# A fused gated-scan and mixture-of-experts kernel on one core: low half 2 moved ahead of VectorE's block turn, the second norm split between GpSimd and ScalarE, and the statistics of x moved behind the tokens' low half

## What is computed

```python
x = x + layernorm(attn(layernorm(x)))        # block 1
x = x + layernorm(ffn(layernorm(x)))         # block 2

# attn: g = sigmoid(x Wg^T + bg); h[l] = (1-g[l])*h[l-1] + g[l]*x[l]; h Wo^T + bo
# ffn:  each token is routed to one of 8 experts, argmax(softmax(x router_w + router_b));
#       an expert takes at most C = 320 of its tokens (rank < C), which get
#       relu(x w1[e] + b1[e]) w2[e] + b2[e];
#       every other token gets relu(x ow1 + ob1) ow2 + ob2
```

## Time and profile before

| | before |
|---|---|
| median of 3 runs (range), us | 1188.42 (1187.62 to 1189.31) |
| the profiled execution's own time, us | 1188.88 |
| its span, first to last instruction, us | 1187.1 |
| TensorE busy | 1137.6 us, 96% of the span |
| TensorE weight loads | 992.1 us, 84% |
| VectorE busy | 985.8 us, 83% |
| ScalarE busy | 744.1 us, 63% |
| GpSimd busy | 706.7 us, 60% |
| mean granted TensorE clock | 0.997 |

### The profile page before, as it was taken

One profiled execution on the slowest core, in us unless ns is written; L12 is line 12 of the kernel. 1 busy time (PEld: TensorE's weight loads), 2 busy tenths in 40 slices (PEclk: granted clock), 3 DMA queues, 4 the chain that ended last, 5 costly groups with the idle time before them and its releaser, 6 DMA issues.

```text
span 1187.1 us, 24579 instructions
## 1 busy us (share of the span) xinstructions
PE 1137.6 (96%) x7341; PEld 992.1 (84%) x7341; DVE 985.8 (83%) x2793; ACT 744.1 (63%) x1375; POOL 706.7 (60%) x792
## 2 busy tenths in 40 slices
PE   8999999999999999999999999999999999999996
PEld 4788888888888888888888888888888888899996
DVE  6888888888888889888888888888988887778885
ACT  4366666666656566666666656666666666678883
POOL 3556666666666656666666666666666655424544
PEclk9999999999999999999999999999999999999998
DMA  9111132222222222222222222222222130245440
GB/s 263 51 45 55 53 104 67 79 56 54 70 71 71 71 71 70 65 68 65 55 66 64 59 54 71 71 71 71 71 66 68 50 100 19 85 139 171 154 131 34
DMA packets 186314, 92.46 MB, mean 78 GB/s; under 512 B 121403, under 2 KB 182509, under 8 KB 186148
## 3 DMA queue, kind: packets, MB, share of 16 engines
q1 hardware_dynamic: 179108, 86.65, 26.1%
q0 software_dynamic: 7168, 5.34, 1.5%
HBM read 53.82 MB, written 38.76 MB: 78 GB/s over the span
## 4 chain that ended last, share of the span: by engine, by line
DVE 43%; PE 31%; issue 11%; another core or an unknown queue 6%; POOL 4%; ACT 3%; DVEq 1%; DMA 0%; POOLq 0%; ACTq 0%
DVE st L917 10%; DVE hid_lo L1081 7%; PE psY L1503 5%; PE psY L1506 5%; PE psY L1505 5%; PE psH L1397 3%; PE psH L1399 3%; PE psH L1398 3%; DVE hst L982 3%; DVE mv L924 3%; DVE ysb L1095 3%; DVE ngx L973 3%; DVE att L988 2%; DVE outt L1011 2%
## 5 line engine op out<-in xcount | busy, mean ns | idle before, releaser
L1503 PE MATMUL psY<-W_hi,hid_hi 128*128 128x256 f32 x1168 | 339.2, 290 | 14.5 <-DVE hid_lo L1081 14.4
L679 ACT ACTIVATE hid<-psH,biasT 128x512 f32<-128x512 f32 (+1 forms) x312 | 202.5, 649 | 222.9 <-PE psH L1399 220.5
L1506 PE MATMUL psY<-W_hi,hid_lo 128*128 128x256 f32 x1168 | 330.4, 283 | 0.0
L1505 PE MATMUL psY<-W_lo,hid_hi 128*128 128x256 f32 x1168 | 330.3, 283 | 0.0
L1503 PEld LDWEIGHTS psY<-W_hi,hid_hi 128*128 128x128 f32 x1168 | 222.8, 191 | 33.9 <-DVE hid_lo L1081 26.7
L1397 PE MATMUL psH<-xfT_hi,W_hi 128*128 128x512 f32 (+1 forms) x624 | 235.9, 378 | 1.6 <-ACT hid L679 1.4
L1398 PE MATMUL psH<-xfT_lo,W_hi 128*128 128x512 f32 (+1 forms) x624 | 235.0, 377 | 0.0
L1399 PE MATMUL psH<-xfT_hi,W_lo 128*128 128x512 f32 (+1 forms) x624 | 232.7, 373 | 0.0
L1505 PEld LDWEIGHTS psY<-W_lo,hid_hi 128*128 128x128 f32 x1168 | 223.1, 191 | 4.9
L1506 PEld LDWEIGHTS psY<-W_hi,hid_lo 128*128 128x128 f32 x1168 | 223.0, 191 | 0.0
L1081 DVE TENSOR_TENSOR hid_lo<-hid,hid_hi 128x512 fp32r<-128x512 f32 (+1 forms) x308 | 199.4, 662 | 25.4 <-ACT hid_hi L684 25.4
(11 more groups left out here) (176 smaller groups left out, 2194.0 us busy)
## 6 DMA issues: line engine op xcount, KB each, us to landing
xin<-L_attn_x SPq DMA_DIRECT2D x32, 512.0 KB, 3.5
stage<-L_ffn_w SPq DMA_DIRECT2D x16, 1024.0 KB, 5.4
out<-outt SPq DMA_DIRECT2D x31, 512.0 KB, 2.8
stage<-L_attn_x SPq DMA_DIRECT2D x26, 512.0 KB, 3.4
stage<-tok SPq DMA_DIRECT2D x416, 32.0 KB
xbuf<-zrow SPq DMA_DIRECT2D x1, 2590.0 KB, 16.2
xin<-xbuf SPq DMA_DIRECT2D x8, 259.0 KB, 5.2
stage<-L_ffn_ow SPq DMA_DIRECT2D x2, 1024.0 KB, 8.4
```

What stands on the lines that cost most here:

```text
L679: act.activation(hid[j % 2][:, at:n], psH[:, j % 2, at:n], ACT.Relu, bias=bias).then_inc(s_hid, 1)
L1503: pe.matmul(dst, hi, w[0][:, j, :], start=(j == 0 and (tail or t % 2 == 0)), stop=False, skip_group_check=True)
L1505: pe.matmul(dst, hi, w[1][:, j, :], start=False, stop=False, skip_group_check=True)
L1506: last = pe.matmul(dst, lo_, w[0][:, j, :], start=False, stop=(j == HC - 1), skip_group_check=True)
```

## The change

The constant `SHARED2` and the function `shared2` name the groups 2 to 30, whose second norm was GpSimd's before. In GpSimd's `norm2` the loop goes over two tiles in place of four. ScalarE gets a `norm2` of its own for the other two, between the high half of slice 6 and the relu of slice 7, with two waits (the deviation, and the transposes of the group before) and a new semaphore, for which `transposes1` waits as well. In VectorE's step, low half 2 stands ahead of `turn_blocks` and `residual2` in place of behind them, and `stats0` stands behind `xf_lo` in place of ahead of low half 7. In `second_step` only the ScalarE part is changed.

```diff
+SHARED2 = 31
+def shared2(g):
+    return not isinstance(g[0], int) or 2 <= 2 * g[0] + g[1] < SHARED2
...
+        s_tok2_act = sem("s_tok2_act")
...
             def norm2(g):
                 i, v = g
                 deviation2(g)
-                if not live(grp(i, v, 1), NG) or not live(grp(i, v, -2), NG):
+                if not shared2(g):
                     return
                 pool.wait_ge(s_nm[2], cnt(g, 1, 1))
                 pool.wait_ge(s_T1, cnt(g, 2, 0))
                 pool.sem_inc(s_held, 1)
-                for t in range(TG):
+                for t in range(TG // 2):
                     last = pool.tensor_scalar(tok2[:, t, :], x1[v][:, t, 0:D], x1[v][:, t, D + 1:D + 2],
                                               x1[v][:, t, D + 2:D + 3], ALU.mult, ALU.add)
                 last.then_inc(s_tok2, 1)
...
+            def norm2(g):
+                v = g[1]
+                if not shared2(g):
+                    return
+                act.wait_ge(s_nm[2], cnt(g, 1, 1))
+                act.wait_ge(s_T1, cnt(g, 2, 0))
+                for t in range(TG // 2, TG):
+                    last = act.activation(tok2[:, t, :], x1[v][:, t, 0:D], ACT.Identity, bias=x1[v][:, t, D + 2:D + 3],
+                                          scale=x1[v][:, t, D + 1:D + 2])
+                last.then_inc(s_tok2_act, 1)
...
                 hidden(range(5, 6))
                 if ahead:
                     sigmoid(far)
-                hidden(range(6, 8))
+                hidden(range(6, 7))
+                if up:
+                    norm2(nxt)
+                hidden(range(7, 8))
                 if up:
                     xf_hi(nxt, GT)
...
-                hidden(6, 7)
+                hidden(6)
+                norm2(nxt)
+                hidden(7)
                 xf_hi(nxt, GT)
...
                 if up:
                     attended(nxt)
                     stats1(nxt)
+                low(2)
                 if ahead and piped(far):
                     turn_blocks(far)
                 if live(grp(i, u, -1), NG):
                     residual2(grp(i, u, -1))
-                low(2)
                 if run and up:
                     place(now)
                 low(3)
...
                 next_x = grp(i, u, 4 if piped(grp(i, u, 3)) else 3)
-                if live(next_x, NG):
-                    stats0(next_x)
                 low(7)
                 if up:
                     xf_lo(nxt, GT)
+                if live(next_x, NG):
+                    stats0(next_x)
...
             def transposes1(g, n, base=0):
                 pe.wait_ge(s_tok2, cnt(g, 1, 1) + base)
                 if base == 0:
+                    if shared2(g):
+                        pe.wait_ge(s_tok2_act, cnt(g, 1, -1))
```

More of the change, by code:

```diff
@@ L66, in sandwich_kernel @@
     NG = N // GT
+    assert NG == SHARED2 + 1
     assert L == 2 * GT and Wg.shape == (D, D) and w1.shape == (E, D, H)
```

## The result

The changed kernel takes 1179.2 us (median of 4, 1179.13 to 1179.27) against 1188.02 (median of 4): ratio 0.9924, 95% interval 0.9907 to 0.9942. It is faster, as forecast, but by 9 us where the forecast said 30, and 1179.2 lies above the range of 1147 to 1173. The profiled execution took 1179.15 us, its span is 1177.3.

The account below looks back on a forecast made before the run. The prediction took TensorE's work (busy 31.0 of 32.1 us a step) as the floor and its three waits as the possible gain. Less new waits, 1.15 us a step over 26 steps made 30 us, so 1158 us, range 1147 to 1173.

Parts of the forecast that it names:

- they cost nothing: VectorE's moved statistics fill its 2.95 us of idling, end 0.8 us ahead of `result`, and delay nothing.
- The three waits: TensorE's waits for low half 2, the scan state's low half and GpSimd's second norm: 1.61 us a step in sum.
- A: TensorE's wait for low half 2 from VectorE: mean 0.735 us a step, expected to go.
- B: TensorE's wait for GpSimd's second norm: 0.31 us a step, of which 0.15 was counted as saved.
- fixed at 2.3 us: VectorE's `result` was taken to start 2.3 us after TensorE's `layer1(0)`, as before the change.
- TensorE alone: Rival, chance 0.2: `result` starts when VectorE is free, saving 1.44 to 1.6 us a step; 1147 to 1151 us.
- the weight of 0.5: The chance given to the forecast's own case, 1152 to 1163 us.
- Left where it was, low half 7 would be late by 0.9: With the statistics still ahead of it on VectorE, low half 7 would reach TensorE 0.9 us late.
- the bound of the sum: GpSimd's `state_lo` ends at 33.7 to 35.1 us; the upper end allows for a held-back first indirect DMA.
- low half 3 as the next wait: TensorE's next wait on VectorE: 0.48 us in every other step, none in the steps between.
- C stays: Rival, chance 0.2: TensorE's wait for the scan state's low half from GpSimd (0.57 us a step) remains.
- The slower rival: Chance 0.07: statistics push `result` to 4.45 us after `layer1(0)`, 25 us slower, 1213 us; deciding from 3.5 on.

Follow-up runs that it names:

- e1: The changed kernel with the two closing instructions of the statistics (`veps`, `nmean`) moved behind `result`: 1146.18 us, ratio 0.9625.
- e2: The changed kernel with GpSimd's `state_lo` made to wait until VectorE has closed the statistics: 1150.76 us, ratio 0.9664.
- e6: The changed kernel with the statistics back in their old place, ahead of low half 7: 1148.05 us, ratio 0.9645.
- e3: The kernel before with low half 2 and the statistics both moved, without the shared second norm: 1240.6 us, ratio 1.0419.
- e4: The kernel before with low half 2 moved ahead of the turn and nothing else: 1180.69 us, ratio 0.9996.
- e7: The kernel before with the second norm shared and nothing else: 1148.18 us, ratio 0.9717.
- e9: e6 with two memsets (1.4 us of idle work) on GpSimd ahead of the fourth indirect DMA: 1149.28 us, ratio 0.9728.
- e12: e1 with one memset of 0.7 us on GpSimd ahead of the fourth indirect DMA: 1160.96 us, ratio 0.9756.
- e5: The kernel before with the statistics moved behind `xf_lo` and nothing else: 1219.97 us, ratio 1.025.

## Why the prediction was wrong in size

**The step that failed is the one on the statistics**, "they cost nothing". It looked at the time in which VectorE idles and at who waits for the statistics, and found both harmless. It took the duration of each instruction over from its old place. In the new place GpSimd's `state_lo` is beside it, and one instruction of 0.17 us takes 2.6. e1 and e2 take the collision away from either side, and 29 to 33 us come back; e6 takes the move away, 31 us. The kernel before has instructions that take longer beside the other engine's: of GpSimd's four tiles from 531.81 on the earlier trace rows the first and the third took 1.54 and 1.95 us, beside scans of VectorE (531.71 to 532.99 and 533.68 to 534.97), and the two others 0.55. Of the moved statistics the forecast didn't ask what they would lie beside.

A slightly earlier start does not spare the instruction: the held `veps` starts 0.04 us ahead of `hst_lo` here (536.65 and 536.69), and 0.42 ahead in e3.

**The three waits don't add up.** The sum counted A, low half 2, as a saving of its own (0.735 us a step, 19 us over 26 steps). e4 removes it and gains nothing. The trace of before, read again as a loop, says why. VectorE's `result` of the first step stood at:

```profile
510.63 1.29 DVE L1095 TENSOR_TENSOR ysb<-psY,ob_b 128x512 f32<-128x512 f32 x2 [2.98 <-remote]
```

From there to the end of GpSimd's tiles (536.37) it is 25.74 us; to the transposes 0.06; to the next `layer1(0)` 3.80; to the next `result` 2.28: 31.88 us, the whole step. TensorE's wait for low half 2 isn't on this loop; VectorE's time for it is, in its old place and in its new one. The wait only decided whether TensorE spends the surplus over its own work before low half 2 or before the transposes. B, with 0.15 us the smallest of the three terms, was the one on the loop, and shortening it (4.56 us of tiles to 1.89) is what made room for everything (e7).

**`result` isn't fixed at 2.3 us** behind `layer1(0)`. Behind the first steps it starts at 0.65 to 1.1 in e6 and e7. The rival "TensorE alone" asked for exactly this and had 1147 to 1151; the sharing alone gives 1148.18. For a kernel without the move of the statistics the weight of 0.5 should have stood there. That the changed kernel still came out somewhat faster than before is in part luck: it is a gain of 33 to 43 us by the sharing (e7 and e6, each against the kernel before on its chip) less a loss of 31 by the move, and the sum had neither.

**"Left where it was, low half 7 would be late by 0.9"** didn't come: behind 245 us neither e6 nor e7 has a wait of TensorE for a low half. With `result` earlier, VectorE has the time; that this is the reason is argued, no run separates it.

**What held:** the sign; the end of the waits for low half 2, for `tok` and for the state; the places of ScalarE's tiles; that the early `dispatch` is held up (1.80 us for its first DMA, inside the bound of the sum); and low half 3 as the next wait. "C stays", with a chance of 0.2, did not come: TensorE's list has no wait for `hst_lo`. The upper end of the range, 1173, stands on no term that a run shows; the 1179.2 above it came of the held `veps`. The wait for low half 3 is 1.1 us in every step instead of 0.48 in every other one, and with it the forecast's own mark of being wrong (more than 1 us) is passed. By steps: 1.15 us forecast, 0.24 found, which over 26 steps is 6 of the 9 us; the rest lies outside the two steps shown. The slower rival, the statistics that push `result`, was right in its place and wrong in its mechanism and price. It had an idle time counted anew from when VectorE gets there; the trace has no idle time, and `result` follows the held instruction at once. The start came at 3.3 to 3.5, its deciding point, and not at 4.45. Without the sharing the hold of `veps` makes the kernel 50 us slower than before (e3).

**What stays open** is what releases `result`. The start lies at 1.6 to 2.5 us behind `layer1(0)` before (but for the 0.2 of the earlier trace rows), at 1.3 to 2.3 in e4, at 1.6 to 1.9 in e1, at 0.65 to 1.1 in e6 and e7, and at 0.2 in e9. A dependence on the fourth DMA is refuted (e9), and no run tells what it is. In e3 and in the changed kernel `result` follows the held instruction at once, so there the loop is closed by the hold. In the kernel before, the last link, from `layer1(0)` to `result`, is read off and not explained; that its period follows GpSimd's tiles is shown by e7.

## What to carry over

Before a short instruction is moved on VectorE, lay GpSimd's instructions of the new place beside it: what costs nothing by its duration can be held beside one (here an instruction of 0.17 us for up to 3.3), and the place is safe only if it stays clear when everything around it becomes faster (e12). Before waits are added up as savings, follow one full period from an instruction to itself; waits on one loop share one surplus, and only what shortens the loop counts. Where a change has several parts, each part alone is a run worth making: here one part gave all (e7), one gave nothing (e4), and one took most of it back (e6 against the changed kernel).

## What was not expected of the hardware

- The hold lasts for a run of GpSimd instructions, not for one. `state_lo` is two subtractions of 1.3 us, and a held instruction ends 0.02 to 0.05 us behind the second in the changed kernel, e1, e3, e5 and e12.
- It begins ahead of the recorded start of `state_lo`, beside the fourth indirect DMA. In e3 `veps` starts at 498.78, 0.42 us ahead of `hst_lo` at 499.20, and is held for 3.04 us. In e5 `nmean` is held when it starts 0.62 us ahead (422.46), and `veps` isn't when it starts 0.70 ahead (422.38). Beside other indirect DMAs the same instructions keep 0.17 us (in e7 `veps` at 426.72, beside the DMA from 426.66). No run separates the end of the fourth DMA from an early start of the hold by `state_lo`.
- It depends on the instruction. Beside the same `hst_lo`, in e1, `result` (one input in PSUM) keeps 1.29 us for its two instructions, while `veps`, with a single SBUF input, is held.
- An indirect DMA directly behind the two tiles took 1.80 us (563.07 to 564.87 in the changed kernel), beside a scan (562.60 to 563.97) and a low half (from 563.89); the three behind it took 0.97 or 0.98. No run separates the scan from the low half.
- The kernel before took 1181 to 1191 us from one chip to the next. The two kernels with the sharing and the statistics in their old place took 1148.05 and 1148.18 on two of these chips, and the changed kernel 1179.2 and 1179.5. Why only the first varies is open.
- In e5 TensorE's waits of 2.09 and 1.8 us for a low half were each followed by a stretch at a lower granted clock (0.50 from 440 to 442 us and from 474 to 476); in e3 waits of up to 1.8 us for `tok` left the mean granted clock at 0.997.
